# Masking the attention weights of the heads: VectorE one head of every second step, in place of both heads of every fourth

## The reference

```python
h = jnp.maximum(_layernorm(x, axis=-1), 0.0)
q = (h @ W_q).reshape(B, N, 4, 32).transpose(0, 2, 1, 3)    # k and v in the same way
scores = jnp.einsum('bhnd,bhmd->bhnm', q, k) / np.sqrt(32)
scores = jnp.where(adj == 0, -jnp.inf, scores)
attn = jax.nn.softmax(scores, axis=-1)
out = jnp.einsum('bhnm,bhmd->bhnd', attn, v)
x = x + (out.transpose(0, 2, 1, 3).reshape(B, N, 128) @ W_o + b_o)
```

## Time and profile before

| | |
|---|---|
| median of 3 runs | 3555.4 us (3553.81 to 3557.63) |
| the profiled execution | 3557.18 us |
| its span, first to last instruction | 3555.3 us |
| mean granted TensorE clock | 0.985 of 2.4 GHz |
| TensorE busy (matmuls) | 3418.1 us, 96% |
| VectorE busy | 3047.1 us, 86% |
| ScalarE busy | 1808.8 us, 51% |
| GpSimd busy | 1834.0 us, 52% |

### The profile page before, as it was taken

The page is one execution under the profiler, slowest core; times in us unless marked ns, Lnnn a source line. Parts: engine busy times, 40 slices in busy tenths (PEclk is TensorE's granted clock), DMA queues, the critical chain, the costliest instruction groups (busy, mean ns, idle before and its releaser), DMA issues. The chain is left out here.

```text
span 3555.3 us, 58165 instructions
## 1 busy us (share of the span) xinstructions
PE 3418.1 (96%) x21155; PEld 1793.6 (50%) x21155; DVE 3047.1 (86%) x6860; ACT 1808.8 (51%) x4044; POOL 1834.0 (52%) x924
## 2 busy tenths in 40 slices
PE   6899998889999999999999999999988999899999
PEld 6899997431111111111111111111126999799999
DVE  8899997579999999999999999999946776577777
ACT  8634442756666666666666666666652544310110
POOL 7300112138888888888888888888880111000000
PEclk9999999999999999999999999999998999999999
DMA  8512122840011001100110011001002332312120
GB/s 300 217 67 90 55 90 84 270 151 18 17 29 30 23 12 29 30 23 12 30 30 23 12 29 29 24 11 29 6 14 99 119 120 82 110 66 78 66 90 25
DMA packets 78816, 234.62 MB, mean 66 GB/s; under 512 B 13504, under 2 KB 40768, under 8 KB 64448
## 3 DMA queue, kind: packets, MB, share of 16 engines
q1 hardware_dynamic: 77808, 230.56, 19.5%
q10 hardware_dynamic: 720, 0.33, 0.0%
HBM read 148.85 MB, written 81.99 MB: 65 GB/s over the span
## 5 line engine op out<-in xcount | busy, mean ns | idle before, releaser
L1803 POOL TENSOR_TENSOR a_w<-a_w,keep_mask_t 128x1024 f32<-128x1024 f32 x768 | 1627.5, 2147 | 298.5 <-ACT a_w L1788 298.5
L1788 ACT ACTIVATE a_w<-a_sc_ps 128x512 f32<-128x512 f32 x2048 | 1111.5, 594 | 713.0 <-PE a_sc_ps L1710 711.4
L1688 PE MATMUL a_o_ps<-a_w,a_v 128*33 128x512 f32 x4096 | 1081.0, 606 | 6.5 <-POOL a_w L1803 6.4
L1175 PE MATMUL g_acc<-g_hv,g_w 128*128 128x129 f32 x8192 | 921.7, 276 | 17.8 <-ACT g_hv L1053 17.8
L1175 PEld LDWEIGHTS g_acc<-g_hv,g_w 128*128 128x128 f32 x8192 | 920.0, 193 | 18.3 <-ACT g_hv L1053 18.2
L1743 DVE CUSTOM_DVE_ANT_0 a_mx_ps<-a_mx_ps,a_mbias 128x512 f32<-128x512 f32 x1024 | 674.6, 719 | 43.2 <-PE a_mx_ps L1672 41.0
L1743 DVE CUSTOM_DVE_ANT_0 a_mx_ps<-a_mx_ps,em_mbias 128x512 f32<-128x512 f32 x968 | 636.8, 719 | 30.0 <-PE a_mx_ps L1672 29.8
L1710 PE MATMUL a_sc_ps<-a_qs,a_ks 97*128 97x512 f16 x2048 | 622.2, 385 | 0.2
L1756 DVE TENSOR_TENSOR a_w<-a_w,keep_mask_t 128x1024 f32<-128x1024 f32 x256 | 453.0, 1770 | 38.7 <-ACT a_w L1788 33.5
L1672 PEld LDWEIGHTS a_mx_ps<-a_ks,a_qs 32*128 32x128 f16 x1992 | 88.8, 91 | 786.9 <-DVE a_mx L1743 428.0
L1020 DVE SCALAR_TENSOR_TENSOR g_w<-f_row,keep_s,keep_mask_t 128x1024 f32<-128x1024 f32 x256 | 322.7, 1281 | 78.3 <-PE g_acc L1175 69.9
(11 more groups left out here) (304 smaller groups left out, 2388.0 us busy)
## 6 DMA issues: line engine op xcount, KB each, us to landing
p_adj_in<-in_adj SPq DMA_DIRECT2D x16, 1024.0 KB, 6.6
v<-p_v SPq DMA_DIRECT2D x32, 264.0 KB, 2.7
a_v<-v SPq DMA_DIRECT2D x16, 528.0 KB, 3.7
f_row<-u_rows SPq DMA_DIRECT2D x16, 512.0 KB, 6.3
g_x<-in_x SPq DMA_DIRECT2D x8, 1024.0 KB, 10.9
g_row<-u_rows SPq DMA_DIRECT2D x16, 512.0 KB, 7.7
x<-g_o SPq DMA_DIRECT2D x16, 512.0 KB, 3.0
a_ks<-k_hi SPq DMA_DIRECT2D x64, 128.0 KB, 2.9
```

Source lines behind the costliest of these rows:

```text
L1175: mm = nc.tensor.matmul(tile(half, it), w[:, g % PB, it * P:(it + 1) * P], hv[:, k, jt, :], start=(jt == 0 and it % 3 == 0), stop=(jt == T ...
L1688: mm = nc.tensor.matmul(o_ps[2 * HD * a:2 * HD * a + HD + 1, c % 2, :], v[u][:, jt, a, :], w[:, g % PB, a, :], start=(jt == 0), stop=(jt = ...
L1788: nc.scalar.activation(w[:, g % PB, a], sc_ps[:, n % SB], ACT.Exp, scale=SCALE).then_inc(exp_done, 1)
L1803: nc.gpsimd.tensor_tensor(w[:, g % PB], w[:, g % PB], keep["mask_t"][:, jt, c * BANK:(c + 1) * BANK].unsqueeze(1).to_broadcast([P, 2, BANK ...
```

## The change

SHARED = 2 takes the place of the list mine. In a step with g % 2 == 1, VectorE masks the second head (w[:, g % PB, 1], 128x512) once both exponentials of the step are done, and GpSimd masks the first (w[:, g % PB, 0], 128x512) once the first exponential is. In the other steps GpSimd masks both heads in one instruction of 128x1024, as it did. So masked_pool now counts every step, masked_dve every second, and the o matmuls of an odd step wait for both.

```diff
-    mine = [g for g in range(BODY) if g % 4 == 1]
+    SHARED = 2
@@ tensor, weigh
-                if g in mine:
-                    pe.wait_ge(masked_dve, len(mine) * i + mine.index(g) + 1)
-                else:
-                    pe.wait_ge(masked_pool, (BODY - len(mine)) * i + g - sum(m < g for m in mine) + 1)
+                if g % SHARED == 1:
+                    pe.wait_ge(masked_dve, (BODY * i + g) // SHARED + 1)
+                pe.wait_ge(masked_pool, BODY * i + g + 1)
@@ vector, mask
-                if g in mine:
+                if g % SHARED == 1:
                     c, jt = g // T % CH, g % T
                     dve.wait_ge(exp_done, 2 * (BODY * i + g + 1) + SB)
-                    nc.vector.tensor_tensor(w[:, g % PB], w[:, g % PB],
-                                            keep["mask_t"][:, jt, c * BANK:(c + 1) * BANK].unsqueeze(1).to_broadcast([P, 2, BANK]),
+                    nc.vector.tensor_tensor(w[:, g % PB, 1], w[:, g % PB, 1], keep["mask_t"][:, jt, c * BANK:(c + 1) * BANK],
                                             ALU.mult).then_inc(masked_dve, 1)
@@ gpsimd
-                    if g in mine:
+                    c, jt = g // T % CH, g % T
+                    if g % SHARED == 1:
+                        pool.wait_ge(exp_done, 2 * (BODY * i + g + 1) + SB - 1)
+                        nc.gpsimd.tensor_tensor(w[:, g % PB, 0], w[:, g % PB, 0], keep["mask_t"][:, jt, c * BANK:(c + 1) * BANK],
+                                                ALU.mult).then_inc(masked_pool, 1)
                         continue
-                    c, jt = g // T % CH, g % T
```

## The result

The changed kernel takes 3587.6 us (median of 4 runs, 3584.65 to 3593.08), the kernel before 3554.61 beside it; the ratio is 1.0093, with a 95% interval of 1.0076 to 1.0111. It is slower by 33 us, outside the range of the prediction. The profiled execution took 3588.14 us and its span is 3586.3, at a granted clock of 0.987.

A forecast was written before the change was run, and what follows sets the result against it. TensorE was taken to bound the heads stage; pace 0, waits 0 and end -1.5 us on the profiled 3557.18 gave 3555.7, lowered to 3554 because the runs' median was 1.8 below the profiled span; range 3549 to 3566.

The forecast's parts named there:

- What bounds the kernel: Heads stage: TensorE sets the pace, 1.84 us a step and 29.44 a chunk, with VectorE and GpSimd close behind.
- The prices: Mask instructions of 128x512 in the heads stage: 1.14 us on GpSimd, 0.68 us on VectorE.
- The turns of two steps: GpSimd's and VectorE's alternating masks: 2.09 + 1.11 + 0.43 = 3.63 us, within TensorE's 3.68.
- The rival that has GpSimd over its limit: Heads stage masks: GpSimd's 512 spacing exceeds 1.16 us, so turns outlast TensorE's pace; up to +32 us, 3586; chance 9%.
- the rival by the harsher rule of the Trainium skill: Heads stage masks: whole instructions exclude each other, 3.95 us for two steps; +138 us, 3692; chance 1%.
- The doubled wait: TensorE's two semaphore waits ahead of odd steps' o matmuls, 512 times: 0.00 us each, at most 5 us in all.
- VectorE's time: VectorE per two steps: 2.65 + 0.68 = 3.33 of 3.68 us, leaving 0.35 to wait for its turn; about 0.33 expected.
- the other order: Mask turns: VectorE finds GpSimd's half tile running, waits for its end, falls into GpSimd's pause; also repeats within 3.68 us.
- my 2.65 us: VectorE's work other than masks in two steps of the heads stage, as half of 5.29 us in four steps.
- the signs I had named: Prediction wrong if: TensorE below 2190 matmul records in 500 us, GpSimd's half tile over 1.19 us, or VectorE releasing o matmuls.
- VectorE out of step: VectorE's mask waits up to 1.97 us behind whole tiles, delaying maxima: 3567 once a batch, 3656 once a chunk; chance 4%.
- The end: Last steps without maxima, bound by masks: shorter turns, 47.2 us against 49.7; taken as -1.5 us, between -3.5 and +2.

The follow-up runs named there:

- Run 6: The changed kernel, but VectorE masks one head of every fourth step only and GpSimd all the rest; 3678.08 us, ratio 1.0350 to the kernel before.
- Run 3: The changed kernel, but GpSimd's half tile also waits until VectorE has masked the other head of the same step; 3683.48 us, ratio 1.0367 to the kernel before.
- run 1: The kernel before, plus a second, already reached GpSimd wait on TensorE ahead of every odd step's o matmuls; 3553.77 us against 3553.23, ratio 1.0001.
- run 9: The changed kernel with even steps shared instead of odd, so no VectorE mask stands ahead of the transposition; 3560.48 us, ratio 1.0017 to the kernel before.
- run 5: The changed kernel, but in the transposition's step (jt = 4) VectorE handles the transposed maxima before its mask; 3559.6 us, ratio 1.0018 to the kernel before.
- run 10: The kernel before, with VectorE's whole tiles in steps g % 4 == 3 instead of 1, one standing ahead of the transposition; 3584.43 us, ratio 1.0085.
- run 11: The kernel before with VectorE's tiles in g % 4 == 3, but transposed maxima handled ahead of the mask at jt = 4; 3553.26 us, ratio 0.9997.
- run 8: The kernel before, but VectorE masks every second step's whole tile in the stage's last 27 steps; 3544.93 us, ratio 0.9976.

## Why the prediction was wrong

**What bounds the kernel: right.** TensorE's pace of 1.84 us a step is the same in every run in which nothing holds it.

**The prices: right.** GpSimd's half tile was put at 1.14 us and has a median of 1.158; VectorE's 128x512 at 0.68, and its least is 0.678. The turns of two steps were put at 3.63 us. Early in the changed kernel, where GpSimd has no pause, its whole tiles start 3.65 us apart (812.00 and 815.65, in the last section). Run 6, where GpSimd is the bound, has 7.855 us in four steps for 7.83. The rival that has GpSimd over its limit was thereby wrong for the change: GpSimd idles before every other tile. That its 3586 us lies beside the measured 3587.6 is chance. Wrong too was the rival by the harsher rule of the Trainium skill (SBUF — State Buffer, section "SBUF: two separate sides"), at full recorded durations 3.95 us for two steps. The trace agrees with the lock (VectorE's mask waits out GpSimd's half tile to its end), but the edges overlap, by about 0.3 us in two steps (2.13 + 1.16 + 0.68 = 3.97 in 3.65). Run 3 is the exception: there a semaphore orders mask and half tile as well, and a round took 3.94.

**The doubled wait: right.** 0.00 us each, by run 1.

**VectorE's time: this step failed.** I wrote that VectorE may wait 0.35 us in each period and would wait 0.33, and that the other order, in which it comes later and finds the half tile running, "also repeats within 3.68". I put no price on VectorE's wait in that order, and nothing on what stands behind it. The trace after is in that order most of the time. The 0.43 us that a VectorE mask was to cost GpSimd is then hardly paid (its half tile takes 1.16 us); VectorE waits instead, 0.52 us (1.20 - 0.68), more than the 0.35 allowed. It does repeat all the same, since a period without the transposition has less other work than my 2.65 us: run 9's masks of 1.18 us follow each other in 3.65 with no pause of VectorE. My 2.65 had spread the chunk's extra work evenly over eight periods. The transposition is not spread. It comes once, TensorE wants its answer within about 1.8 us, and in the new order of VectorE's queue a mask that waits 0.5 us stands ahead of it. That was 33 us, where the sum had nothing. I did list what is queued behind TensorE's new wait, and not what is queued behind VectorE's longer ones. Runs 5, 9, 10 and 11 show that the place is the cause: the order gives back 28 of 33 us, the parity 27, and the kernel before loses 30 us when its own masks are put there and none when the small operation goes first. Of the signs I had named, the first came (2151 matmul records in 500 us); the half tile stayed under 1.19 us, and VectorE did not become what o matmuls wait for.

**The rival "VectorE out of step"** had the right engine and, in its second case, the right rate (once a chunk), at 1.6 us instead of 0.56, since I took it for a wait behind a whole tile after a large delay. Half a microsecond of lateness was enough. With 4% it had far too little weight.

**The end: the number right, by luck.** I had -1.5 us. The stage's first and last o matmuls are 1884.2 us apart before (771.1 to 2655.3) and 1917.7 after (769.1 to 2686.8), 33.5 us more. The last transpositions divide them:

```profile
2599.83 0.27 PE L1667 MATMUL a_mx_ps<-keep_ident,a_mrow 128*8 128x128 f32 x1
```

```profile
2632.72 0.27 PE L1667 MATMUL a_mx_ps<-keep_ident,a_mrow 128*8 128x128 f32 x1
```

From there to the last o matmul it is 55.5 us before and 54.1 after, so the end gave 1.4 us; the pauses took 59 x 0.56 = 33.0 and the rest of the stage 1.9. But I had reckoned with shorter turns at an unchanged drop of the clock. In fact TensorE's waits for masks in the end grew, from 6.4 to 7.4 us, and the clock did not drop (1.00 from 2600 to 2690), which is worth about the 3 us of run 8.

**What stays open.** The last 6 us of run 9. (Those of run 5 are the 0.10 us in each chunk.) Run 9 has none in the profiled execution and about 6 us in the others, so something differs from one execution to the next. It may be the order of turns, but with one profile that is not shown.

## What to carry to other kernels

When an edit moves or lengthens an instruction on an in-order engine, list what comes right behind it and who needs that by when; a mean load per period does not see an operation that comes once in sixteen steps and has a deadline. A rare operation on a handshake belongs ahead of bulk work that can wait, above all ahead of work that has to wait for its turn at a shared path: it then costs next to nothing, since it runs within that wait (run 11; run 5 but for its 0.10 us a chunk). And if the work of one engine ends earlier than the stage (VectorE's maxima here), its share of the rest can grow there; that was worth 9 us. Last, an engine's busy share counts its waits for the shared path. It was 99% with the loss and 99% in run 5, nearly without it, and 97% in run 10, which loses too.

## What the runs showed of the hardware

- The engines do not meet at semaphores alone, as I wrote at the start: a VectorE product of two SBUF tensors and a GpSimd one take turns. With nothing but the shared path between them, a half tile of VectorE costs about 0.44 us of GpSimd's time (half tiles of 1.60 us in place of 1.16 where they follow at once), less than its 0.68. With a semaphore from one to the other, the round costs nearly the sum of the full durations (3.94 us, by run 3).
- In one and the same kernel the turns can settle in different orders, half tile first or VectorE first, and stay so for several steps. For some 25 us early in the changed kernel GpSimd's half tiles take 1.60 us, VectorE having gone first; in most of the stage they take 1.16, as in the timeline at 1342.06 above. GpSimd's timeline in the early part:

```profile
812.00 2.13 POOL L1804 TENSOR_TENSOR a_w<-a_w,keep_mask_t 128x1024 f32<-128x1024 f32 x1
814.08 1.61 POOL L1800 TENSOR_TENSOR a_w<-a_w,keep_mask_t 128x512 f32<-128x512 f32 x1
815.65 2.13 POOL L1804 TENSOR_TENSOR a_w<-a_w,keep_mask_t 128x1024 f32<-128x1024 f32 x1
```
- In the kernel before, TensorE waited 0.50 us and then 1.57 us near the end, and for the next three steps the clock was granted at the 1.2 GHz level, wholly or in part (o matmuls of 1.92, 1.92 and 1.41 us in place of 1.05, 0.80 over the 10 us of the earlier trace rows). Not every wait had this effect: 1.22 us some 12 us before them had not, nor had thirteen waits of 7.4 us in all at the end of the changed kernel, most of them near 0.54 us. With the waits gone (run 8), the window is at 1.00.
